# Two of four leading products of zeros replaced by 32-row transposes and rounded products in row tiles

## The reference

```python
q = (x @ Wq.T).reshape(b, n, NUM_HEADS, HEAD)
k = (x @ Wk.T).reshape(b, n, NUM_HEADS, HEAD)
v = (x @ Wv.T + bv).reshape(b, n, NUM_HEADS, HEAD)
bias = (spatial_encoding + edge_encoding)[:, None]      # adj + adj
scores = jnp.einsum('bqhd,bkhd->bhqk', q, k) * scale + bias
row_nonzero = jnp.any(scores != 0, axis=-1, keepdims=True)
p = jax.nn.softmax(jnp.where(row_nonzero, scores, -jnp.inf), axis=-1)
out = jnp.einsum('bhqk,bkhd->bqhd', jnp.nan_to_num(p), v).reshape(b, n, h)
x = _layernorm(x + out @ Wo.T + bo)
```

## Time and profile before

| | us |
|---|---|
| median of 3 runs | 660.97 |
| the runs | 660.78, 660.97, 662.17 |
| profiled execution, its own time | 661.33 |
| profiled execution, span from first to last instruction | 659.5 |
| PE busy in the span | 638.3 |
| mean granted TensorE clock, share of full speed | 0.999 |

### The profile page before, as it was taken

The page is one execution under the profiler, slowest core; times in us unless marked ns, Lnnn a source line. Parts: engine busy times, 40 slices in busy tenths (PEclk is TensorE's granted clock), DMA queues, the critical chain, the costliest instruction groups (busy, mean ns, idle before and its releaser), DMA issues.

```text
span 659.5 us, 18322 instructions
## 1 busy us (share of the span) xinstructions
PE 638.3 (97%) x6060; PEld 550.3 (83%) x6060; DVE 502.6 (76%) x2319; ACT 517.6 (78%) x1942; POOL 410.4 (62%) x500
## 2 busy tenths in 40 slices
PE   9999999999999999999999999999999999999774
PEld 5788888888888888888888888888888888888673
DVE  4667887877887777887877887777877877877884
ACT  5678887878878788877878878788877878877782
POOL 1557665756756666765766856666765756845662
PEclk9999999999999999999999999999999999999999
DMA  9300312121121210212121131210212111011111
GB/s 306 122 4 9 106 57 105 57 74 44 48 105 58 104 50 19 95 59 104 58 86 41 38 106 58 104 50 29 85 58 105 57 50 36 32 58 58 49 49 49
DMA packets 17951, 45.88 MB, mean 70 GB/s; under 512 B 1984, under 2 KB 7104, under 8 KB 17856
## 3 DMA queue, kind: packets, MB, share of 16 engines
q1 hardware_dynamic: 17424, 44.11, 19.3%
q10 hardware_dynamic: 432, 0.59, 0.3%
HBM read 32.11 MB, written 12.58 MB: 68 GB/s over the span
## 4 chain that ended last, share of the span: by engine, by line
PE 67%; POOL 16%; issue 8%; DVE 7%; ACT 2%; POOLq 0%
PE qk_ps L279 21%; PE vo_ps L357 11%; POOL tree L230 10%; PE vo_ps L311 10%; PE pt_ps L325 9%; PE scores_ps L296 6%; PE att_ps L342 5%; DVE nscores L498 4%; POOL x_t L212 4%; PE pt_ps L332 2%; ACT probs L409 2%; PE scores_ps L369 1%; PE pt_ps L265 1%; POOL x_n L219 1%; DVE att_t L538 1%
## 5 line engine op out<-in xcount | busy, mean ns | idle before, releaser
L409 ACT ACTIVATE probs<-nscores,neg_max 128x128 f32<-128x128 f32 x768 | 296.7, 391 | 3.1 <-DVE neg_max L498 3.1
L498 DVE CUSTOM_DVE_ANT_0 nscores<-scores_ps,adj_n 128x128 f32<-128x128 f32 x768 | 171.6, 286 | 16.0 <-PE scores_ps L296 16.0
L409 ACT ACTIVATION_READ_ACCUMULATOR probs<-nscores,neg_max 128x1 f32 x768 | 146.5, 191 | 0.0
L230 POOL TENSOR_TENSOR tree<-nscores 128x768 f32<-128x768 f32 x64 | 120.2, 1878 | 36.0 <-DVE neg_max L498 36.0
L325 PE MATMUL pt_ps<-ident,probs 128*128 128x128 f32 x768 | 118.7, 277 | 9.2 <-ACT probs L409 7.0
L357 PE MATMUL vo_ps<-w_o,att_t 128*128 128x384 f32 x576 | 116.8, 347 | 0.0
L212 POOL TENSOR_TENSOR x_t<-x_raw,x_t 128x512 fp32r<-128x512 f32 x45 | 58.4, 1300 | 93.5 <-ACT x_t L426 93.5
L311 PE MATMUL vo_ps<-w_v,x_t 128*128 128x384 f32 x576 | 114.1, 342 | 0.0
L325 PEld LDWEIGHTS pt_ps<-ident,probs 128*128 128x128 f32 x768 | 89.8, 140 | 28.9 <-ACT probs L409 7.9
L230 POOL TENSOR_TENSOR tree<-tree 128x384 f32<-128x384 f32 (+1 forms) x128 | 103.8, 811 | 10.0
L279 PE MATMUL qk_ps<-x_t,w_k 128*128 128x512 f32 x405 | 105.4, 404 | 2.6 <-POOL x_t L212 2.6
(11 more groups left out here) (56 smaller groups left out, 808.2 us busy)
## 6 DMA issues: line engine op xcount, KB each, us to landing
x_n<-xn SPq DMA_DIRECT2D x32, 384.0 KB, 3.6
out<-out_n SPq DMA_DIRECT2D x32, 384.0 KB, 2.6
x_raw<-xt SPq DMA_DIRECT2D x15, 768.0 KB, 5.4
adj_n<-adj SPq DMA_DIRECT2D x32, 128.0 KB, 2.0
x_raw<-xt SPq DMA_DIRECT2D x3, 256.0 KB, 5.5
nscores<-wq ACTq DMA_DIRECT2D x3, 192.0 KB, 4.2
nscores<-wk SPq DMA_DIRECT2D x3, 192.0 KB, 5.5
probs<-wv SPq DMA_DIRECT2D x1, 576.0 KB, 6.4
```

The source lines that it names most:

```text
L230: nc.gpsimd.tensor_tensor(tree[:, b % 2, :, 0:width], src[:, :, 0:width], src[:, :, width:2 * width], ALU.add).then_inc(tree_step, 1)
L409: last = nc.scalar.activation(probs[:, b % 2, h], nscores[:, b % 2, h], ACT.Exp, bias=neg_max[:, b % 2, h:h + 1], scale=-1.0, accum_out=ro ...
L498: last = nc.vector.tensor_tensor_reduce(out=nscores[:, half, h], in0=scores_ps[j][:, m * P:(m + 1) * P], in1=adj_n[:, b // 2 % 2, half], s ...
```

## The change

The four leading products of zeros become two. Behind them PE waits for the identity and then issues 8 rounds of 4 transposes, each of a 32x128 piece of `zeros` against the 32x32 diagonal block of `ident`, and 8 rounds of 4 rounded (float32r) products of a 32x128 piece of the new tile `zeros_r` with itself. Within a round the four operations use four different row tiles of the array and four different PSUM banks (`scores_ps[0..3]`). Nobody reads the results, and the first real products overwrite the banks. DVE gets a second memset, of `zeros_r` (128x128), and PE now waits for both memsets before its first product.

```diff
@@ -50,6 +50,7 @@
         zeros = sb("zeros", [P, 512])
+        zeros_r = sb("zeros_r", [P, P], F32R)
         x_raw = sb("x_raw", [P, 2, KT, GRP * P])
@@ -359,8 +360,18 @@
-            pe.wait_ge(zeroed, 1)
-            run_idle(4)
+            pe.wait_ge(zeroed, 2)
+            run_idle(2)
+            pe.wait_ge(ident_step, 2)
+
+            for turned_over in (True, False):
+                for _ in range(8):
+                    for j in range(HPT):
+                        rows = slice(j * D, (j + 1) * D)
+                        if turned_over:
+                            nc.tensor.transpose(scores_ps[j][:, 0:D], zeros[rows, 0:P], ident[rows, rows])
+                        else:
+                            nc.tensor.matmul(scores_ps[j][:, 0:P], zeros_r[rows], zeros_r[rows], start=True, stop=True)
             for k in range(KT):
                 pe.wait_ge(first_split, 3 * k + 3)
@@ -552,6 +563,7 @@
             nc.vector.memset(zeros[:], 0.0).then_inc(zeroed, 1)
+            nc.vector.memset(zeros_r[:].bitcast(F32), 0.0).then_inc(zeroed, 1)
```

## The result

| | before | changed |
|---|---|---|
| median, us | 661.1 (660.52 to 662.82) | 663.16 (660.76 to 664.3) |
| executions | 20 | 20 |
| profiled execution, us | 661.33 | 664.3 |
| its span, us | 659.5 | 662.5 |

The ratio is 1.0024 with a 95% interval of 1.0016 to 1.0031: the change makes the kernel slower by about 0.24%, 2 us by the medians. The changed kernel's times are not a cloud around one value: four of the 20 lie at 660.8 to 661.9, like before, and 14 between 662.6 and 663.6. Two lie at 664.3, and the profiled execution is one of them, so its rows show more loss than the median has.

What follows compares the result with a forecast made beforehand. PE was taken to bound the kernel, busy for 638.3 of 659.5 us. The warm-up, 5.36 + 0.20 + 2.36 = 7.92 against 7.70, ends 0.2 us later, giving 661.2 us, range 660.4 to 663.5.

Steps and rivals of the forecast that it cites:

- rival A: Start of PE work: clock rises late, first real products run slow, 662.4 to 664.8 us, most likely near 663; chance 0.25.
- the likeliest case: Warm-up on PE ends 0.2 us later and the whole kernel shifts so: 661.2 us, own range 660.8 to 661.9; chance 0.50.
- if the clock rises at about 6.6 as before: Warm-up on PE: assumed the step from 1.2 to 2.4 GHz stays at about 6.6 us, before any real product.
- A's price: First real products on PE: 0.2 us more for each at the lower clock; six of them 1.2 us, 18 3.6.
- A's reason: Warm-up on PE: 32-row operations, half of them transposes, may not lift the clock; a skill rule says transposes don't engage it.
- The sum of the warm-up: End of the warm-up on PE: 5.36 + 0.20 + 2.36 = 7.92 us, against 7.70 before.
- The price of 0.037 for every small operation: The 64 small warm-up operations: 0.037 us each, taken from the scores; 1.18 us for each kind.
- the floor of 0.033: Small warm-up operations: lowest cost per operation in the trace, from the attention row; half of 0.037 was not excluded.
- The 0.20 for the change of tiles: Ahead of the small operations: 0.20 us for PE's change from full height to row tiles.
- B: Small warm-up operations don't overlap or have a floor of 0.073 us each: warm-up 2.6 us late, 663.5 us; chance 0.10.
- The cap of 0.38 on a gain: Third query copy on DVE: an earlier warm-up end can gain at most 0.38 us, since DVE is next to limit.
- I take the shift there to pass whole to the end.: From 21 us on, PE's own results release everything, so any shift at the first scores reaches the kernel's end in full.

Runs made afterwards that it cites:

- the control: The changed kernel timed once more, nothing altered, beside the kernel before: 663.22 us, ratio 1.0026.
- `turned_only`: The changed kernel with 88 transposes of 32 rows in place of its 64 small operations: 662.58 us, ratio 1.0017 to the kernel before.
- `rounded_only`: The changed kernel with 52 rounded 32-row products in place of its 64 small operations: 663.01 us, ratio 1.0020 to the kernel before.

## Why the prediction was right or wrong

*Direction and size.* 661.2 was forecast, 663.16 came: a loss of 0.2 us against one of 2. It is inside the range and at the time that rival A was given (near 663), but A had a chance of 0.25 and the likeliest case was another; the range held because it took in A. The step that failed is the one on the clock: "if the clock rises at about 6.6 as before". It rose between 9.5 and 10.6 in the profile, and the first 12 real products took 1.27 us longer for it. "The clock is the real question" was right; the row that was lacking was one of 32-row work ahead of a rise, and without it the likeliest case leaned on the work being dense.

*A's price.* 0.2 us for each real product at the lower level, "about six": measured 12 products in 4.07 against 2.80, 1.27 us, which is six or seven times 0.2.

*A's reason.* Half wrong. The diff's 32 rows were named as one reason and the transposes as the other, with the Trainium skill's rule behind the second. Full height cleared both kinds; what was left is the small 32-row form of the two together, and for each kind alone a loss at the start was not seen in a profile.

*The sum of the warm-up.* Forecast 7.92, measured 8.12 (5.36 + 1.00 + 1.76). The end of the two products, 5.36, and the second memset, 1.57 - 1.43 = 0.14 for 0.15, were exact. The price of 0.037 for every small operation was mis-sized in both directions: transposes 0.027 (32 from 5.29 to 6.16), rounded products 0.059 at the lower level (32 from 6.16 to 8.05) and 0.032 at the higher. Nor was the floor of 0.033 one: with transposes alone and the clock up, 88 took 1.50 us (5.18 to 6.68), 0.017 each. The 0.20 for the change of tiles did not appear: zeros end at 5.35, the first transpose starts at 5.29. Letting the level and the shorter work cancel was fair for the transposes, not for the products.

*B.* Fell: no floor of 0.073, and the operations overlap: 0.059 for a rounded one of 32 rows, 0.18 for one of full height (nine in 1.66).

*The cap of 0.38 on a gain.* Right in kind, not in size: with the clock up early the rounded 32-row run started its real products at 6.77, and its last ended at 19.63 (18.77 + 0.86), 0.68 before the 20.31 of the earlier trace rows. DVE set the pace there, as forecast: the `w_o` step and the three query copies stood without a gap, the third at 19.80. The first scores at 20.62 are 0.55 before, more than the cap: the `w_o` step took 1.36 in place of 1.72 and ended 0.08 earlier (18.68 for 18.76), and the third copy started 0.08 before the second is printed as ended. With transposes alone that step started at 17.34 in place of 17.04 and took 1.72, and the scores came at 21.00, 0.17 before: the cap was not a fixed number.

*"I take the shift there to pass whole to the end."* Nearly: in the control 1.67 us of shift at the first scores became 1.4 of span. And it missed a second term at the end, the fall of the clock behind PE's pauses, which cost the profiled execution another 1.4 us (6.68 in place of 5.25 from the last transposes to the start of the last output projection). I had read the end as untouched since its code was, and it is not: the first profile and the control's are of one kernel, one with the fall and one without.

## What to carry to other kernels

Work that only keeps TensorE warm should look like the full-height work it stands in for: on this kernel 2.8 us of 128-row products and transposes ahead of the first real product kept its speed, and the same time of small 32-row operations did no better than idling and was in the way as well. Judge such edits at the start by how many real products run at the lower level, and at the end by the pauses ahead of the last dense work. Where times fall into groups, one profile shows one group; more executions and a control of the same kernel are needed before its rows explain a median. The mean granted clock of each execution costs nothing and sorts them by what no single profile shows. And an edit at the end of a program can't take credit for a change that its profile shows at the start.

## What the runs showed of the hardware

- Float32 transposes of 128x128 were as good as products for the clock: real products behind 14 of them started at full speed, 661.66 us in all, ratio 1.0000 to the kernel before.
- 32-row operations in four row tiles cost 0.027 us (transposes) and 0.059 us (rounded products, 128 columns) each at the lower level, 0.017 (`turned_only`) and 0.032 (`rounded_only`) at the higher.
- In the changed kernel's profile the granted clock fell to 0.50 for the stretch from 648.70 to 652.10 after two pauses of 1.32 and 0.88 us that left PE busy for 1.58 of 3.40 us, while the same two pauses passed without a fall in the profiles of the kernel before (busy for 1.61 of 3.40 us) and of the control. With the pauses filled, one of 34 executions had a mean clock of 0.996 or less; without, 15 of 30 of the changed kernel.
- The clock rose near 5 us in some profiled executions and near 10 in others of programs with the same first 5 us.
